# Chunk update of a recurrent layer: loops written out, the first slab's terms formed one step earlier, next terms in front of a slab's transposes, unread products left out

## The chip, the cores and the metric

The kernel runs on 1 core of one Trainium2 chip. The metric is the device time of one execution in microseconds (us). Before the change it is 9437.5 us, the median of three runs (9432.24, 9437.5 and 9437.68).

## What is computed

A small audio tower: a token layer, an attention layer, a feed-forward layer with top-k selection, a recurrent layer and a layer of experts, each added to a residual. The change touches the recurrent layer alone. Cut to what matters:

```python
def _mlp(params, z):
    W0, W1, P0, P1 = params
    h = z @ W0 + z @ P0
    h = jax.nn.silu(h)
    return h @ W1 + h @ P1
...
def step(carry, xs):
    cp, cm = carry
    k_t, v_t, q_t, a_t, th_t, e_t = xs
    g = jax.vmap(jax.grad(loss_fn))(cp, k_t, v_t)
    s = lambda c: c[:, :, None]
    nm = jax.tree_util.tree_map(lambda m, gg: m * s(e_t) - s(th_t) * gg, cm, g)
    np_ = jax.tree_util.tree_map(lambda p, m: p * (1.0 - s(a_t)) + m, cp, nm)
    out_t = jax.vmap(_mlp, in_axes=(0, 0))(np_, q_t)
    new_carry = jax.lax.stop_gradient((np_, nm))
    return (new_carry, out_t)
...
h = h + _L1_attn_ref(_layernorm(h, axis=-1), ...)
```

Each of 249 time steps takes a gradient of a two-layer network with respect to its own weights, updates momentum and weights with it, and evaluates the new network. All in float32.

## The kernel before, in words

The function recurrent_layer (L1801 on) doesn't update the weights at every step. It cuts the 249 steps into 16 chunks, 15 of 16 steps and a last one of 9. Within a chunk, a step works with the weights as they stood at the chunk's start and adds the contribution of the chunk's earlier steps from a history (tile hist: h, y and slope rows of the steps so far). At the start of the next chunk an **update** folds the whole history into weights and momentum. So the program is: update, 16 steps, update, 16 steps, and so on. All engines have their own instruction list for this and meet by counting semaphores: V counts what VectorE (DVE) has finished, T TensorE (PE), A ScalarE (ACT), P GpSimd (POOL). Each has a fixed number of counts per update and per step, so a wait is "V has reached the count of sn of slab 3 of chunk c".

The update goes over 16 slabs X, each of two halves k:

- DVE weighs history rows for a group of two slabs (weighed, L2503, tile wy, which lies in the buffer named hdiag), PE multiplies them with the history (new_terms, L2266, into the banks psNew, two pairs used in turn; a wait at its start asks for the sn of slab X - 2).
- DVE updates the slab with the result: sa (L2521), sb (L2527), sn (L2531), two instructions each, and between slabs makes the tables of decay factors for the chunk (beside, L2465 to L2498).
- PE turns the updated slab over (turned, L2282, transposes into the banks psC), and ACT copies it to where the steps read it (L2192).
- After slabs 4, 6, 8 and 10, PE forms base values for the steps from the chunk's slopes (from_last, L2305 in chunk 0, L2307 later), ACT copies them (L2200), SP and POOL store them (L2055). When all are stored, SP loads the first step's two base rows back (load_base, L2026 and L2027).
- After slab 12 PE turns the decay tables over (L2317, L2326). From these DVE makes cu (L2539), which the next chunk's update reads, then x0 from the two base rows (L2541), the first hidden activations (L2546, ACT's sigmoid L2204, L2551), PE turns them over (turn, L2336), DVE places them on a diagonal (L2556), and the first step's products begin (L2350).

PE issues the slabs in the order: transposes of X, from_last if there is one, new terms of X + 2. In front of each slab's transposes stands one product that nobody reads (kept_warm, L2250, 256 columns, into a psC bank); two more of 512 columns stand behind the last copy wait of the update and two more behind the definition of the step, ahead of the first turn (four in a row in the list).

A step is bound by PE: products with the chunk's weights (L2350), with the history, and backwards (L2403). Its last part on DVE is slope(0) and slope(1) (L2623, L2625, L2630, and L2634, which writes tile dl); SP copies h, y and dl of each step to the history in eight transfers each (to_hist, L2038) and stores y (L2160).

DVE's chunks 0 to 14 are one loop on the chip (Fori) and chunk 15 is written out behind it. PE has chunk 0, a loop over chunks 1 to 8, one over 9 to 14, and chunk 15. In a chunk, 15 steps are a loop and the last step is written out.

Of the kernel before, what the change touches and what calls it, by code (L numbers as in the profile page):

```python
# [7 lines left out]
ALU = mybir.AluOpType  # L8
# [7 lines left out]
CH, NCH = 16, 16  # L16
# [1766 lines left out]
def recurrent_layer(nc, CT, DXD, VR, GR, YR, BASED, BASEO, W0, P0, W1, P1):  # L1783
# [8 lines left out]
    with ExitStack() as ctx:  # L1792
# [3 lines left out]
        def sem(name):  # L1796
            return ctx.enter_context(nc.semaphore(name))
# [67 lines left out]
        psC, psBase, psOld = (b[6], b[0]), (b[3], b[4]), b[1][:, HD:]  # L1865
        psNew = ((b[5], b[7]), (b[1], b[2]))

        def slab(X, k):
# [7 lines left out]
                  5: ["rep0", "rep1"], 6: ["d3a", "d3b", "d3c"], 13: ["cm", "cmx"]}  # L1876
        vec_u = ["wy0"]
        for X in range(16):
# [11 lines left out]
        for X in range(16):  # L1890
            pe_u += [f"tr{X}0", f"tr{X}1"] + ([f"nb{X // 2 - 2}"] if X in NB else []) + ([f"nw{X + 2}"] if X < 14 else []) + (["ct", "cb"] if X == 12 else [])
        pe_s = ["tr", "pred", "gt", "yp", "yt", "ob", "a", "dd", "dt", "dha", "e", "tra", "dhb"]
# [8 lines left out]
        old_in = [Stages(sem(f"old_in{nb}"), [], ["in"], 16 * (1 + 2 * nb), first) for first, last, nb in PARTS]  # L1901
        old_out = Stages(sem("old_out"), [], ["out"], 16)
        slopes_out = Stages(sem("slopes_out"), ["out"], [], 8 * 16)
        ctn_in = Stages(sem("ctn_in"), ["in"], [], 8 * 16, 1)
# [9 lines left out]
        hist_d = Stages(sem("hist_d"), [], ["d"], 16 * NH)  # L1914
        for q in (*old_in, old_out, slopes_out, ctn_in, first_in, *base_out[0], *base_out[1], gates_in, cc_in, al_in, base_in, value_in, hist_h, hist_y, hist_d):
            q.base = 0
# [152 lines left out]
        with nc.Block() as block:  # L2069
# [173 lines left out]
            def _(e):  # L2243
                def chunk(c, steps, part):
# [6 lines left out]

                    def new_terms(X):

                        G = X // 2
                        e.wait_ge(V.sem, V.upd(c, f"wy{G}"))
                        if X == 0:

                            e.wait_ge(hist_h.sem, c * (hist_h.unit * CH))
                        if X >= 2:

                            e.wait_ge(V.sem, V.upd(c, f"sn{X - 2}1"))
                        for w in range(2):
                            for k in range(2):
                                j, m, g, n = slab(X, k)
                                rows = slice(32 * g, 32 * g + 32)
                                mm = e.matmul(psNew[X % 2][k][:, HD * w:HD * w + HD], wy[rows, G % 2, w, :, :].rearrange("p u d -> p (u d)"),  # L2266
                                              hist[rows, m * 4 + j, 0:HD], start=True, stop=True)
                        mm.then_inc(T.sem, 1)

                    def turned(X):  # L2270
                        for k in range(2):
                            if X:
                                e.wait_ge(A.sem, A.upd(c, f"c{X - 1}{k}1"))
                            if k == 0:
                                kept_warm(psC[k], 1, 256)
                        for k in range(2):
                            j, m, g, n = slab(X, k)
                            e.wait_ge(V.sem, V.upd(c, f"sn{X}{k}"))
                            for hf in range(2):
                                for w in range(2):  # L2280
                                    o = 256 * hf + 128 * w
                                    mm = e.transpose(psC[k][:, o:o + 128], mvt[:, 4 * n + j, HD * w + 128 * hf:HD * w + 128 * hf + 128], ident[:, :])  # L2282
                            mm.then_inc(T.sem, 1)

                    def from_last(q):
# [22 lines left out]
                        mm.then_inc(T.sem, 1)  # L2308

                    e.wait_ge(V.sem, V.begun(c))  # L2310
                    e.wait_ge(A.sem, A.begun(c))
                    settled(e, s_pe)
                    new_terms(0)
                    new_terms(1)
                    for X in range(16):
                        turned(X)
                        if X in NB:  # L2317
                            from_last(X // 2 - 2)
                        if X < 14:
                            new_terms(X + 2)  # L2320
                        if X == 12:
                            e.wait_ge(V.sem, V.upd(c, "d3c"))
                            e.wait_ge(A.sem, A.upd(c, "bs7"))
                            settled(e, s_pe)
                            for w in range(2):
                                mm = e.matmul(psCT[:, 128 * w:128 * w + 128], rep[:, w, :, :].rearrange("p i s -> p (i s)"), ident[:, :],  # L2326
                                              start=True, stop=True)
                            mm.then_inc(T.sem, 1)
                            for w in range(3):
                                mm = e.matmul(psH[:, 128 * w:128 * w + 128], ones[:, :], d3[w], start=True, stop=True)  # L2330
                            mm.then_inc(T.sem, 1)
                    e.wait_ge(A.sem, A.upd(c, "c1511"))
                    kept_warm(psC[0], 2)
                    def turn(hf, need):
# [95 lines left out]

                    kept_warm(psC[0], 2)
                    e.wait_ge(T.sem, T.upd(c, "cb"))
# [4 lines left out]
                    with e.Fori(0, steps - 1) as s:  # L2437
                        step(s, False)
                    step(steps - 1, True)

                chunk(0, CH, 0)
                for part in (1, 2):
                    with e.Fori(*PARTS[part][:2]) as c:
                        chunk(c, CH, part)
                chunk(NCH - 1, LAST, 3)

            @block.vector
            def _(e):
# [3 lines left out]
                def chunk(c, steps):  # L2452
# [48 lines left out]
                    def weighed(G):  # L2501
                        j, m = G // 2, G % 2
                        go(e.tensor_tensor(wy[:, G % 2, :, :, :],  # L2503
                                           hist[:, m * 4 + j, HD:HD + D].unsqueeze(1).unsqueeze(1).to_broadcast([128, 2, 2, D]),
                                           cmx[:, :, j, m, :].unsqueeze(3).to_broadcast([128, 2, 2, D]), ALU.mult), f"wy{G}")
# [64 lines left out]
                    def step(s, last):  # L2570
# [49 lines left out]
                        def slope(hf, names, need):  # L2620
# [34 lines left out]

                with e.Fori(0, NCH - 1) as c:
                    chunk(c, CH)
                chunk(NCH - 1, LAST)

# [81 lines left out]
```

## Time and profile before

| | before |
|---|---|
| runs, us | 9432.24, 9437.5, 9437.68 |
| profiled execution: its own time, us | 9434.71 |
| profiled execution: span from first to last instruction, us | 9432.9 |
| PE busy | 8531.5 us, 90% of the span |
| DVE busy | 4381.6 us, 46% |
| ACT busy | 1955.9 us, 21% |
| mean granted clock of TensorE | 0.951 |

The recurrent layer takes some 6.45 ms of the span: the first new terms start at 1944.9 us (L2266), the last chunk's first step at 8209.4 us. One chunk is some 412 to 417 us long, of which the update, from the last dl of one chunk to the first L2350 of the next, is 60.5 to 64.4 us in chunks 1 to 14, and 56.4 us in chunk 15.

### The profile page before, as it was taken

Reading aid. Unit: us, or ns where it says so; the run is one execution under the profiler, and the core shown is the slowest. Engines: PE = TensorE matmul, PEld = TensorE weight load, DVE = VectorE, ACT = ScalarE, POOL = GpSimd, SP = SyncE. Lnnn points to the kernel's source line nnn. Section 1 sums busy time; section 2 is a strip of 40 time slices with the busy share of each in tenths; the row PEclk is TensorE's granted clock in tenths of the full one; section 3 lists DMA queues with packets and bytes.
Section 4 is the critical chain, followed back from the end, with each engine's and each line's share of the span. In section 5 each row is a group of like instructions: output and inputs, shape, how many; then the busy total and the mean of one; then the engine's idle time right before and its main releaser. Section 6 shows DMA issues by size and latency. Waiting matters only on the chain. (4 is left out here: it accounts for less than half of the span.)

```text
span 9432.9 us, 368730 instructions
## 1 busy us (share of the span) xinstructions
PE 8531.5 (90%) x152997; PEld 5630.7 (60%) x152997; DVE 4381.6 (46%) x12189; ACT 1955.9 (21%) x4831; POOL 684.5 (7%) x844
## 2 busy tenths in 40 slices
PE   6888847679999999999999999999999999989999
PEld 2555515356667676666767666676767667653333
DVE  5455578853443444344344434434443444432222
ACT  1344425111111111111111111111111111113333
POOL 0000043110000000000000000000000000000000
PEclk8899966989999999999999999999999999989999
DMA  4000001721221212122122212222222222210000
GB/s 166 20 4 5 4 9 54 157 58 30 59 61 54 59 57 58 55 60 60 55 59 57 58 55 78 79 84 79 81 77 85 78 72 85 68 28 10 14 14 8
DMA packets 800576, 531.23 MB, mean 56 GB/s; under 512 B 277694, under 2 KB 789590, under 8 KB 797990
## 3 DMA queue, kind: packets, MB, share of 16 engines
q1 hardware_dynamic: 769046, 456.94, 17.6%
q0 software_dynamic: 30992, 67.51, 2.5%
q8 instruction: 289, 4.73, 0.2%
q14 instruction: 249, 2.04, 0.1%
HBM read 311.32 MB, written 175.89 MB: 52 GB/s over the span
## 5 line engine op out<-in xcount | busy, mean ns | idle before, releaser
L2350 PE MATMUL bank<-mv,hdiag 128*32 128x144 f32 x63744 | 2050.5, 286 | 9.9 <-DVE hdiag L2556 5.9
L2350 PEld LDWEIGHTS bank<-mv,hdiag 128*32 128x32 f32 x63744 | 1932.8, 110 | 88.7 <-DVE hdiag L2556 11.4
L2403 PE MATMUL bank<-mvt,ydiag 128*32 128x256 f32 x31872 | 1946.9, 381 | 0.0
L2403 PEld LDWEIGHTS bank<-mvt,ydiag 128*32 128x32 f32 x31872 | 1048.0, 110 | 565.5 <-issue 3.3
L2204 ACT ACTIVATE work<-work 128x128 f32<-128x128 f32 x498 | 154.4, 310 | 2211.7 <-DVE work L2546 2209.6
L2590 DVE TENSOR_TENSOR rep<-bank,ta 128x128 f32<-128x128 f32 x249 | 72.7, 292 | 994.9 <-PE bank L2350 994.9
L617 DVE TENSOR_REDUCE att_mx<-att_bank 124x2 f32<-124x496 f32 x512 | 334.0, 664 | 344.8 <-PE att_bank L422 344.8
L2623 DVE TENSOR_SCALAR work<-bank,ta 128x128 f32<-128x128 f32 x498 | 174.8, 351 | 592.0 <-PE bank L2403 592.0
L2192 ACT ACTIVATE mv<-bank 128x256 f32<-128x256 f32 x1024 | 313.7, 388 | 632.5 <-PE bank L2282 632.3
L2077 POOL MEMSET hdiag<- 128x1124 f32 x16 | 16.6, 1035 | 5391.0 <-DVEq L2647 5381.0
L2266 PE MATMUL bank<-hist,hdiag 32*128 32x256 f32 x2048 | 310.6, 456 | 97.3 <-DVE hdiag L2503 97.3
L1425 ACT ACTIVATE moe_hw<-moe_bank 128x496 f32<-128x496 f32 x512 | 271.2, 581 | 610.1 <-PE moe_bank L1339 610.0
L536 ACT ACTIVATE att_ex<-att_bank 124x496 f32<-124x496 f32 x512 | 283.8, 581 | 540.1 <-PE att_bank L434 540.1
L1473 DVE TENSOR_TENSOR moe_xc<-moe_xT,moe_bank 128x496 f32<-128x496 f32 x128 | 86.0, 672 | 620.4 <-PE moe_bank L1348 620.4
L2219 ACT ACTIVATE yth<-ydiag 64x32 f32 (+1 forms) x498 | 131.1, 263 | 1124.2 <-PE bank L2396 1112.9
L2214 ACT ACTIVATE mv<-hdiag 128x128 f32 (+1 forms) x249 | 106.3, 427 | 1219.9 <-PE bank L2350 1219.9
L2282 PE MATMUL bank<-r_ident,mvt 128*128 128x128 f32 x2048 | 297.3, 293 | 22.5 <-DVE mvt L2531 22.4
L422 PE MATMUL att_bank<-att_ka,att_qn 32*124 32x496 f32 x1024 | 293.4, 646 | 20.7 <-DVE att_mx L617 8.4
L2371 PE MATMUL bank<-hist,adiag 128*32 128x256 f32 x3984 | 309.4, 381 | 0.0
L2282 PEld LDWEIGHTS bank<-r_ident,mvt 128*128 128x128 f32 x2048 | 262.0, 152 | 67.8 <-DVE mvt L2531 41.4
L2266 PEld LDWEIGHTS bank<-hist,hdiag 32*128 32x128 f32 x2048 | 187.7, 213 | 179.2 <-issue 89.1
L1337 PE MATMUL moe_bank<-moe_xc,moe_w1T 64*128 64x496 f32 x1024 | 293.4, 636 | 0.8 <-DVE moe_xc L1473 0.8
(417 smaller groups left out, 11813.6 us busy)
## 6 DMA issues: line engine op xcount, KB each, us to landing
ring<-between_slopes SPq DMA_DIRECT2D x320, 512.0 KB, 4.1
baset<-between_base_old SPq DMA_DIRECT2D x265, 128.0 KB, 2.1
baset<-between_base SPq DMA_DIRECT2D x265, 128.0 KB, 2.2
hist<-h SPq DMA_DIRECT2D x1992, 8.0 KB
hist<-y SPq DMA_DIRECT2D x1992, 2.0 KB
hist<-dl SPq DMA_DIRECT2D x1992, 8.0 KB
between_base_old<-bo SPq DMA_DIRECT2D x240, 128.0 KB
ct<-between_table SPq DMA_DIRECT2D x320, 64.0 KB, 2.0
```

The source lines that it names most:

```text
L422: e.matmul(bank[i % 2][0:TL, 0:2 * L], qn[rows, t.buf(1), TL * a:TL * a + TL], ka[rows, t.buf(1), :, :], start=True, stop=True).then_inc(T ...
L536: e.activation(ex[:, t.buf(0), TILE_HEAD[i], :, :], bank[2 + i % 2][0:TL, 0:2 * L].rearrange("p (m n) -> p m n", m=2), ACT.Exp).then_inc(A ...
L617: e.tensor_reduce(mx[:, a, 32 * g + 16:32 * g + 18], bank[i % 2][0:TL, 0:2 * L].rearrange("p (h m) -> p h m", h=2), AX, ALU.max).then_inc( ...
L1337: e.matmul(dst[q], w1T[rows[q], x_, half], xc[rows[q], (I // 2) % 2, :], start=True, stop=False)
L1425: e.activation(hw[:, I % 4, q, :], bank[2 + 2 * (I % 2) + q][:, 0:2 * L], ACT.Relu).then_inc(A.sem, 1)
L2192: e.activation(dst, src, ACT.Copy).then_inc(A.sem, 1)
L2266: mm = e.matmul(psNew[X % 2][k][:, HD * w:HD * w + HD], wy[rows, G % 2, w, :, :].rearrange("p u d -> p (u d)"), hist[rows, m * 4 + j, 0:HD ...
L2282: mm = e.transpose(psC[k][:, o:o + 128], mvt[:, 4 * n + j, HD * w + 128 * hf:HD * w + 128 * hf + 128], ident[:, :])
L2350: mm = e.matmul(psP[32 * j:32 * j + 32, 0:MW], hdiag[:, hf, r, j, :], mv1[:, hf, r, j, :], start=(hf == 0 and r == 0), stop=(hf == 1 and r ...
L2371: mm = e.matmul(psA[32 * j:32 * j + 32, :], adiag[:, m, j, :], hist[:, m * 4 + j, HD + D:], start=(m == 0), stop=(m == 1))
L2403: mm = e.matmul(psBack[hf][32 * j:32 * j + 32, :], ydiag[:, n, j, :], both, start=(n == 0), stop=(n == 7))
L2623: nm(e.tensor_scalar(dh[:, half], S2, W16, None, ALU.mult))
```

## The change

It makes four edits to recurrent_layer.

1. The chunk loops of PE and DVE are written out in Python: c is a constant in each of 16 copies of the chunk. The loops over steps stay. ACT, POOL and SP are as before.
2. The next chunk's first weighed rows are formed in the last step of a chunk, in front of slope(0), behind a wait for ACT's copy of h and for the last y rows and the y store to have landed. They have a semaphore of their own (first_rows). PE forms new_terms(0) of the next chunk at the end of its list for the last step, and the two pairs of psNew banks are swapped.
3. In the update the new terms of X + 2 stand in front of the transposes of X, and from_last behind them.
4. All calls of kept_warm are gone. The transposes of X wait once for the last copy of X - 1, where two waits stood, one for each half.

```diff
-        psNew = ((b[5], b[7]), (b[1], b[2]))
+        psNew = ((b[1], b[2]), (b[5], b[7]))
...
                     def turned(X):
-                        for k in range(2):
-                            if X:
-                                e.wait_ge(A.sem, A.upd(c, f"c{X - 1}{k}1"))
-                            if k == 0:
-                                kept_warm(psC[k], 1, 256)
+                        if X:
+                            e.wait_ge(A.sem, A.upd(c, f"c{X - 1}11"))
...
+                    if part == 0:
+                        new_terms(0)
                     e.wait_ge(V.sem, V.begun(c))
                     e.wait_ge(A.sem, A.begun(c))
                     settled(e, s_pe)
-                    new_terms(0)
                     new_terms(1)
                     for X in range(16):
+                        if X < 14:
+                            new_terms(X + 2)
                         turned(X)
                         if X in NB:
                             from_last(X // 2 - 2)
-                        if X < 14:
-                            new_terms(X + 2)
...
                     e.wait_ge(A.sem, A.upd(c, "c1511"))
-                    kept_warm(psC[0], 2)
...
-                    kept_warm(psC[0], 2)
...
                     step(steps - 1, True)
-
-                chunk(0, CH, 0)
-                for part in (1, 2):
-                    with e.Fori(*PARTS[part][:2]) as c:
-                        chunk(c, CH, part)
-                chunk(NCH - 1, LAST, 3)
+                    if c + 1 < NCH:
+                        e.wait_ge(A.sem, A.begun(c + 1))
+                        e.wait_ge(hist_h.sem, (c + 1) * (hist_h.unit * CH))
+                        new_terms(0, c + 1)
+
+                for first, last, part in (*PARTS, (NCH - 1, NCH, 3)):
+                    for c in range(first, last):
+                        chunk(c, CH if c + 1 < NCH else LAST, part)
...
+                    if c == 0:
+                        weighed(0)
                     e.wait_ge(T.sem, T.begun(c))
                     e.wait_ge(A.sem, A.begun(c))
-                    e.wait_ge(hist_y.sem, c * (hist_y.unit * CH))
-                    weighed(0)
...
+                        if last and c + 1 < NCH:
+                            e.wait_ge(A.sem, A.step(c, s, "ht"))
+                            e.wait_ge(hist_y.sem, (c + 1) * (hist_y.unit * CH))
+                            weighed(0)
                         slope(0, ("dh1a", "dh2a", "dh3a", "da"), "dha")
...
-                with e.Fori(0, NCH - 1) as c:
-                    chunk(c, CH)
-                chunk(NCH - 1, LAST)
+                for c in range(NCH):
+                    chunk(c, CH if c + 1 < NCH else LAST)
```

How the order of the instructions moves, at three places. A row is a line of the kernel, an operation, its tiles and its shape; REGISTER_ALU rows compute the value of a wait, and ISA rows are waits and semaphore counts.

DVE, from a chunk's last slope to the next chunk's first slab, before (dl is the slope's result, L2503 the weighed rows, L2521 the first sa):

```order
L2630 TENSOR_TENSOR work<-work,bank 128x128
L2450 REGISTER_ALU
L2634 TENSOR_TENSOR dl<-work 128x128
L2450 REGISTER_ALU
L2647 ISA
L2656 REGISTER_ALU
L2656 COMPARE_AND_BRANCH
L2503 TENSOR_TENSOR hdiag<-hist,cmx 128x256
L2521 SCALAR_TENSOR_TENSOR mvt<-mvt,cu,bank 128x256 x2
L2503 TENSOR_TENSOR hdiag<-hist,cmx 128x256
L2527 SCALAR_TENSOR_TENSOR mvt<-mvt,cu 128x256 x2
```

The same place in the changed kernel, from the last step's slope(0) on (L2637 writes dl, L2524 is the first sa):

```order
L2621 TENSOR_TENSOR ddiag<-bank,mi 128x8x2x8
L2502 TENSOR_TENSOR hdiag<-hist,cmx 128x256
L2626 TENSOR_SCALAR work<-bank,ta 128x128
L2628 SCALAR_TENSOR_TENSOR work<-bank,ta,work 128x128
L2633 TENSOR_TENSOR work<-work,bank 128x128
L2637 TENSOR_TENSOR dl<-work 128x128
L2646 ISA
L2626 TENSOR_SCALAR work<-bank,ta 128x128
L2628 SCALAR_TENSOR_TENSOR work<-bank,ta,work 128x128
L2633 TENSOR_TENSOR work<-work,bank 128x128
L2637 TENSOR_TENSOR dl<-work 128x128
L2654 ISA
```

The weighed rows have moved from behind the loop's branch to a place two slopes earlier, and sa follows the last ISA row with no branch and no weighed rows between.

PE, from a chunk's last products backwards into the next update, before (chunk 15's copy, which stands behind the loop; L2266 are new terms, four products to a slab, L2250 the unread product, L2282 the transposes):

```order
L2403 MATMUL bank<-mvt,ydiag 32x256 x8
L2443 REGISTER_ALU
L2443 COMPARE_AND_BRANCH
L2443 UNCONDITIONAL_BRANCH
L2443 ISA
L2311 ISA
L2255 REGISTER_ALU
L2258 REGISTER_ALU
L2266 MATMUL bank<-hist,hdiag 128x256 x8
L2250 MATMUL bank<-yth,r_ident 128x256
L2278 REGISTER_ALU
L2282 MATMUL bank<-r_ident,mvt 128x128 x4
```

And now, at any chunk's end:

```order
L2401 MATMUL bank<-mvt,ydiag 32x256 x32
L2267 MATMUL bank<-hist,hdiag 128x256 x12
L2280 MATMUL bank<-r_ident,mvt 128x128 x8
L2267 MATMUL bank<-hist,hdiag 128x256 x4
L2280 MATMUL bank<-r_ident,mvt 128x128 x8
L2267 MATMUL bank<-hist,hdiag 128x256 x4
L2280 MATMUL bank<-r_ident,mvt 128x128 x8
```

The new terms of slabs 0, 1 and 2 now stand ahead of the first transposes (twelve products in one row), those of X + 2 ahead of the transposes of X, and the row of the unread product and the register rows are gone.

PE, from the update's last transposes to the first step, before (L2336 is the turn of h, L2350 the step's first products):

```order
L2282 MATMUL bank<-r_ident,mvt 128x128 x4
L2332 REGISTER_ALU
L2250 MATMUL bank<-yth,r_ident 128x512 x4
L2432 ISA
L2335 REGISTER_ALU
L2336 MATMUL bank<-r_ident,h 128x128
L2435 REGISTER_ALU
L2437 UNCONDITIONAL_BRANCH
L2437 ISA
L2343 ISA
L2350 MATMUL bank<-mv,hdiag 32x144 x44
```

And now:

```order
L2267 MATMUL bank<-hist,hdiag 128x256 x4
L2280 MATMUL bank<-r_ident,mvt 128x128 x24
L2334 MATMUL bank<-r_ident,h 128x128
L2434 UNCONDITIONAL_BRANCH
L2434 ISA
L2341 ISA
L2348 MATMUL bank<-mv,hdiag 32x144 x44
```

Between the last transposes and the turn of h stands nothing any more.

## Rows read from the trace of the kernel before

**Rows 1.** The page's busy times: engine, busy us, share of the span, instructions.

```profile
PE 8531.5 (90%) x152997; PEld 5630.7 (60%) x152997; DVE 4381.6 (46%) x12189; ACT 1955.9 (21%) x4831; POOL 684.5 (7%) x844
```

**Rows 2.** PE by line and shape: busy us, mean ns, idle before and its releaser.

```profile
L2266 PE MATMUL bank<-hist,hdiag 32*128 32x256 f32 x2048 | 310.6, 456 | 97.3 <-DVE hdiag L2503 97.3
L2282 PE MATMUL bank<-r_ident,mvt 128*128 128x128 f32 x2048 | 297.3, 293 | 22.5 <-DVE mvt L2531 22.4
L2250 PE MATMUL bank<-yth,r_ident 128*128 128x256 f32 x512 | 196.1, 468 | 5.0 <-ACT mv L2192 5.0
L2307 PE MATMUL bank<-hist,hdiag 32*32 32x256 f32 x1920 | 65.5, 380 | 0.0
```

**Rows 3.** DVE by line and shape, same columns.

```profile
L2503 DVE TENSOR_TENSOR hdiag<-hist,cmx 128x256 f32<-128x256 f32 x128 | 53.6, 419 | 51.1 <-issue 49.7 <-PEq L1932 0.9 <-DVEq L2647 0.5
```

**Rows 4.** Timeline, chunk 2 to 3: start us, us, engine, line, operation [idle before <-releaser].

```profile
3174.43 0.35 DVE L2623 TENSOR_SCALAR work<-bank,ta 128x128 f32<-128x128 f32 x1 [1.60 <-PE bank L2403]
...
3176.47 0.37 SPq L2160 DMA_DIRECT2D between_recurrent<-y  x1
...
3179.83 0.29 DVE L2634 TENSOR_TENSOR dl<-work 128x128 f32<-128x128 f32 x1
...
3183.64 0.42 DVE L2503 TENSOR_TENSOR hdiag<-hist,cmx 128x256 f32<-128x256 f32 x1 [3.51 <-issue]
...
3184.20 2.11 PE L2266 MATMUL bank<-hist,hdiag 32*128 32x256 f32 x16 [5.52 <-DVE hdiag L2503]
...
3186.31 0.87 DVE L2521 SCALAR_TENSOR_TENSOR mvt<-mvt,cu,bank 128x256 f32<-128x256 f32 x2 [2.25 <-PE bank L2266]
...
3188.76 1.97 PE L2282 MATMUL bank<-r_ident,mvt 128*128 128x128 f32 x8 [1.30 <-DVE mvt L2531]
...
3190.66 2.07 PE L2266 MATMUL bank<-hist,hdiag 32*128 32x256 f32 x8
...
3192.66 1.22 PE L2250 MATMUL bank<-yth,r_ident 128*128 128x256 f32 x2
```

**Rows 5.** Timeline, chunk 14 to 15, which DVE enters without a branch back.

```profile
8153.03 0.29 DVE L2634 TENSOR_TENSOR dl<-work 128x128 f32<-128x128 f32 x1
...
8153.79 0.43 DVE L2503 TENSOR_TENSOR hdiag<-hist,cmx 128x256 f32<-128x256 f32 x1 [0.46 <-DVEq L2647]
...
8155.45 0.87 DVE L2521 SCALAR_TENSOR_TENSOR mvt<-mvt,cu,bank 128x256 f32<-128x256 f32 x2 [1.24 <-PE bank L2266]
```

**Rows 6.** Stretches: us, busy PE, PEld, DVE, ACT, POOL, PE clock, DMA share, GB/s.

```profile
3186.31:3221.05 34.74, 33.44 (x278) 23.50 (x279) 31.76 (x89) 15.59 (x46) 8.88 (x16) 0.85 0.21 45
8155.45:8188.63 33.18, 31.01 (x278) 21.62 (x279) 31.68 (x89) 15.48 (x46) 11.96 (x22) 0.95 0.23 50
3183.24:3196.65 13.41, 11.15 (x50) 7.73 (x52) 9.81 (x30) 2.63 (x8) 7.82 (x15) 0.50 0.22 28
8159.65:8163.06 3.41, 3.41 (x14) 2.19 (x10) 3.41 (x9) 0.81 (x3) 2.86 (x6) 0.50 0.40 31
```

**Rows 7.** Timeline, PE in two slabs of chunk 3 at full clock.

```profile
3204.78 1.13 PE L2266 MATMUL bank<-hist,hdiag 32*128 32x256 f32 x8
...
3207.35 1.13 PE L2266 MATMUL bank<-hist,hdiag 32*128 32x256 f32 x8
```

**Rows 8.** Timeline, end of chunk 3's update and its first step.

```profile
3236.29 0.43 DVE L2541 TENSOR_TENSOR xb<-baset 128x256 f32<-128x256 f32 x1
...
3237.58 3.70 PE L2250 MATMUL bank<-yth,r_ident 128*128 128x512 f32 x8 [0.86 <-ACTq L2231]
...
3238.05 0.29 DVE L2551 TENSOR_TENSOR h<-work 128x128 f32<-128x128 f32 x1 [0.85 <-ACT work L2204]
...
3241.11 0.27 PE L2336 MATMUL bank<-r_ident,h 128*128 128x128 f32 x1
...
3242.03 2.90 PE L2350 MATMUL bank<-mv,hdiag 128*32 128x144 f32 x88 [0.64 <-DVEq L2566]
```

**Rows 9.** What the 16 instructions of L2541 waited for: us, times.

```profile
  DMA baset<-between_base: 3.4, 4
```

More of the change, by code:

```diff
@@ L1876, in recurrent_layer @@
                   5: ["rep0", "rep1"], 6: ["d3a", "d3b", "d3c"], 13: ["cm", "cmx"]}
-        vec_u = ["wy0"]
+        vec_u = []
         for X in range(16):
@@ L1890, in recurrent_layer @@
         for X in range(16):
-            pe_u += [f"tr{X}0", f"tr{X}1"] + ([f"nb{X // 2 - 2}"] if X in NB else []) + ([f"nw{X + 2}"] if X < 14 else []) + (["ct", "cb"] if X == 12 else [])
+            pe_u += ([f"nw{X + 2}"] if X < 14 else []) + [f"tr{X}0", f"tr{X}1"] + ([f"nb{X // 2 - 2}"] if X in NB else []) + (["ct", "cb"] if X == 12 else [])
         pe_s = ["tr", "pred", "gt", "yp", "yt", "ob", "a", "dd", "dt", "dha", "e", "tra", "dhb"]
@@ L1902, in recurrent_layer @@
         old_out = Stages(sem("old_out"), [], ["out"], 16)
+        first_rows = Stages(sem("first_rows_weighed"), ["wy0"], [])
         slopes_out = Stages(sem("slopes_out"), ["out"], [], 8 * 16)
@@ L1914, in recurrent_layer @@
         hist_d = Stages(sem("hist_d"), [], ["d"], 16 * NH)
-        for q in (*old_in, old_out, slopes_out, ctn_in, first_in, *base_out[0], *base_out[1], gates_in, cc_in, al_in, base_in, value_in, hist_h, hist_y, hist_d):
+        for q in (*old_in, old_out, first_rows, slopes_out, ctn_in, first_in, *base_out[0], *base_out[1], gates_in, cc_in, al_in, base_in, value_in, hist_h, hist_y, hist_d):
             q.base = 0
@@ L2250, in kept_warm, with new_terms @@
                             e.matmul(out[:, 0:cols], ident[:, :], yth[:, :, :].rearrange("p a s -> p (a s)")[:, 0:cols], start=True, stop=True)
-                    def new_terms(X):
+                    def new_terms(X, c=c):
                         G = X // 2
-                        e.wait_ge(V.sem, V.upd(c, f"wy{G}"))
-                        if X == 0:
-                            e.wait_ge(hist_h.sem, c * (hist_h.unit * CH))
+                        if G == 0:
+                            e.wait_ge(first_rows.sem, c + 1)
+                        else:
+                            e.wait_ge(V.sem, V.upd(c, f"wy{G}"))
                         if X >= 2:
@@ L2502, in weighed @@
                         j, m = G // 2, G % 2
-                        go(e.tensor_tensor(wy[:, G % 2, :, :, :],
-                                           hist[:, m * 4 + j, HD:HD + D].unsqueeze(1).unsqueeze(1).to_broadcast([128, 2, 2, D]),
-                                           cmx[:, :, j, m, :].unsqueeze(3).to_broadcast([128, 2, 2, D]), ALU.mult), f"wy{G}")
+                        ins = e.tensor_tensor(wy[:, G % 2, :, :, :],
+                                              hist[:, m * 4 + j, HD:HD + D].unsqueeze(1).unsqueeze(1).to_broadcast([128, 2, 2, D]),
+                                              cmx[:, :, j, m, :].unsqueeze(3).to_broadcast([128, 2, 2, D]), ALU.mult)
+                        if G == 0:
+                            ins.then_inc(first_rows.sem, 1)
+                        else:
+                            ins.then_inc(V.sem, 1)
+                    if c == 0:
+                        weighed(0)
                     e.wait_ge(T.sem, T.begun(c))
                     e.wait_ge(A.sem, A.begun(c))
-                    e.wait_ge(hist_y.sem, c * (hist_y.unit * CH))
-                    weighed(0)
                     for X in range(16):
```

## The prediction

> **What bounds the kernel now.** I read the page's busy times first: PE is busy for 90% of the span and every other engine for under half [rows 1]. That share is mostly the steps, which the change leaves alone. So I looked for what the update waits for, chunk by chunk, in the views by line, the timeline, and the busy time of single stretches.
>
> The first wait is at each chunk's start. By line, the weighed rows L2503 have 49.7 us of idle DVE in front of them that nothing in the profile ends, "issue" [rows 3]. It is in 14 places, so 3.55 us each. In chunk 3 it stands between dl and the weighed rows, 3.51 us; PE waits 5.52 us in all, its products begin at 3184.20, and the first sa starts 6.48 us after dl began (3186.31 less 3179.83) [rows 4]. Chunk 15, which DVE enters without a branch back, has 0.46 us in that place and 2.42 us from dl to sa [rows 5]. So I read the 3.5 us as the loop's jump; the rest is the weighed rows, the new terms, and a half clock.
>
> The second is the pace of the slabs. From sa of slab 0 to sn of slab 10 chunk 3 takes 34.74 us and chunk 15 33.18, and DVE is busy for 31.76 and 31.68 of them, PE for 33.44 and 31.01 [rows 6]. Both engines are nearly full. In chunk 3 the granted clock was 0.50 from 3183.24 to 3196.65, after PE's idle time; in chunk 15, after a shorter idle time, only from 8159.65 to 8163.06 [rows 6]. At half clock a slab costs PE 2.07 + 1.22 + 1.97 = 5.26 us [rows 4]; at full clock slabs follow each other after 2.57 us [rows 7].
>
> The third is the end of the update. The hidden activations h are written by 3238.34, but PE stands in four unread products for 3.70 us, turns h at 3241.11, and starts the step at 3242.03 [rows 8].
>
> **The change part by part**, for one chunk, then times the chunks. The sum is made against the profiled execution, 9434.7 us, which is 2.8 us under the median.
>
> *Loops written out, first terms formed early.* The jump, the weighed rows and PE's new terms leave the way from dl to sa. What is left is dl itself (0.29) and DVE's sequence of about 0.46, as in chunk 15 [rows 5]: 0.8 against 6.48, so 5.7 less. Against that stands the new wait. The y store of the last step is issued until 3176.84, while slope(0) began at 3174.43 [rows 4]; the weighed rows and slope(0) behind them now start when the store has landed, and with slope(0) 1.6 us and wy 0.42 long slope(1) may be pushed. The trace has no such wait. Its bounds are 0 (slope(1) waits for PE until 3178.74 anyway) and 1.5 us (landing 1.5 us after issue). I take 0.5. PE is not held up: in the last step its own list waits for no slope. So 5.2 less, in 14 chunks 73 us. Chunk 15 had no jump and gains 2.42 less 1.3, 1 us.
>
> *Unread products between slabs, and the order of terms and transposes.* The 512 rows of unread products cost 196.1 us [rows 2], 0.77 us in each of 256 slabs, 1.22 at half clock [rows 4]. Without them PE needs 2.1 us a slab at full clock (terms 1.13 [rows 7], transposes half of 1.97 [rows 4]; the means of [rows 2], 1.21 and 1.16 for eight rows, mix both levels), and DVE becomes the limit: 31.7 us busy for these eleven slabs. The gain is then at most 34.74 less 31.7, 3 us a chunk. At half clock PE needs 4.04 us a slab, 1.2 less than before, but it stays the limit, and each further slab at half clock costs 4.04 less 2.57, 1.5 us, and every from_last another 1.1 (65.5 us in 60 groups [rows 2]). So the two ends of this term are 3 us less, and, were all eleven slabs at half clock, 11 x 4.04 + 4 x 2.18 = 53.2 us against 34.74, 18 us more. What decides is for how long the clock stays down. In the trace it came back after three slabs with the unread products in them, with PE full. I take a stretch two slabs and one from_last longer: 3 x 1.2 less, 2 x 1.5 + 1.1 more, about 0. It is nearest to the row of 13.41 us at 0.50.
>
> The Trainium skill speaks against this part: "TensorE: Matmul & The Clock Gate" says in its section on what matters for kernels that gaps in PE's work bring the clock back to its lower level, and in Part 4 that transposes don't count as work in the same way. In this kernel an idle time of 5.5 us was indeed followed by a half clock [rows 4, 6]; on transposes no row here separates them.
>
> *Base rows.* Slabs that run faster bring x0 nearer to the chain from_last, ACT's copy, store, load. L2541 waited for that load in 4 of 16 chunks already [rows 9], and from_last now stands behind one more set of new terms (1.1 us). So what DVE gains behind slab 10 is lost at x0; I take 0.6 more, with ends 0 and 2: 8 us.
>
> *Unread products at the end.* With h there at 3238.34 and 0.92 us from turn to step as now, the step would start at 3239.3 in place of 3242.03 [rows 8]: 2.7 less in each of 16 chunks, 43 us. The cover that they gave is gone: PE is idle from the last transposes to the step, some 3 us but for the turn, and the clock may be down at the step's start. One stretch at half clock was 3.41 us long [rows 6] and would lose 1.7 us of a full PE; bounds are 0 and two stretches, 3.4. I take 2.2, 35 us. So of this part little is left.
>
> *Two waits in one, register rows, swapped banks.* The second copy's wait is the later one, and covered by DVE's pace: nothing. The ISA rows of PE's list lie in front of waits: nothing. Between the ends of POOL's and SP's lists nothing moves; POOL's clearing of a buffer is released by dl as before, and read after slab 0.
>
> Sum: -73 - 1 + 0 + 8 - 43 + 35 = -74, and 9434.7 - 74 = 9360.7; I say **9361 us**, 0.8% faster.
>
> **The rivals.**
>
> *Full clock, DVE as the limit.* PE's idle time at the boundary falls from 5.5 us to one or two, and the clock may hardly fall. For it: chunk 15 lost one stretch of 3.41 us alone [rows 6]. Against: it had the unread products. Then slabs go as in chunk 15, 34.74 less 33.18, 1.6 us, in 14 chunks 22 us, up to 3 in the best case, and the step's start loses nothing (35): -74 - 22 - 35, or about 9304 us. Chance 0.23.
>
> *Half clock through the update: slower.* The place is PE from slab 0 on. Without the unread products it has gaps in each slab while DVE sets the pace, and once the clock is down it needs all its time for 4.04 us a slab. For it: in the trace the clock was at 0.50 for 13.41 us even with the unread products. Against: at half clock PE is full, as it was when the clock rose. If the half clock lasts for all slabs, the term is up to 18 us a chunk in place of 0; with two thirds of it, 12 in 15 chunks, it is 180 us: 9541. It decides from 5 us a chunk on (74 over 15): with 1.5 us a slab and 1.1 for every second one, that is two or three slabs more at half clock than the five I took, some eight of sixteen. Chance 0.15; the cases about that point, where gain and loss cancel, have 0.11. By the skill's rule on gaps and transposes this rival would be the likely one.
>
> *The end's gain is given back at x0.* If the base rows land two us later than DVE could use them, the term of 0.6 becomes 2: 20 us more, 9381. For it: four waits already [rows 9]. Chance 0.1, on the same side.
>
> *The jump stays in another form.* A list twice as long might stall DVE once a chunk at its start as the loop's branch did, 3.5 us x 14 = 50 us: 9411. Against it: chunk 15's start is straight code, and had 0.46 us [rows 5]. Chance 0.05. The Trainium skill, "Runtime: NRT & Kernel Launch", section on instruction fetch, says that a taken branch outside the window already fetched stalls, and straight code is fetched ahead; chunk 15's start agrees.
>
> **How the numbers follow.** The forecast has a chance of 0.36, full clock 0.23, x0 0.10, the jump 0.05, the cancelling case 0.11, half clock 0.15. A measurement of this kernel tells some 0.2% from no change, 19 us. Faster by more than that are the first four, 0.74; the same 0.11; slower 0.15. The range of 8 in 10 runs from 9295, a little beyond the full clock case, to 9450, which takes in the cancelling case and leaves the half clock outside.
>
> **What would show it.** Right: no idle DVE over 1 us between the last dl and sa of slab 0; new terms of slab 0 done ahead of dl; from dl to the first product of a step about 57 us where it was 62.2; h turned within half a us of its writing. The clock's rows at the boundary show which case holds: 0.50 for some five slabs is mine, 1.00 the first rival, 0.50 up to slab 15 the second. Wrong: idle DVE in front of sa that PE ends over many slabs, sn of slab 10 over 38 us behind the first sa, an L2350 group of a step's start at half clock for more than two stretches, or a last dl over 1.5 us late.

## The result, and the profile after

The changed kernel takes 9616.95 us (median of four runs, 9602.86 to 9626.0) against 9434.87 us (four runs, 9424.21 to 9437.68): a ratio of 1.0194, with a 95% interval of 1.0176 to 1.0211. It is slower by 182 us where 74 us less were forecast. The profiled execution took 9626.0 us, its span is 9624.5 us, and its mean granted clock 0.907, where it was 0.951.

The page's busy times of the changed kernel, to set beside [rows 1]:

```profile
PE 8738.3 (91%) x152357; PEld 5747.5 (60%) x152357; DVE 4377.2 (45%) x12189; ACT 1975.4 (21%) x4831; POOL 683.8 (7%) x844
```

PE executes 640 instructions fewer (the 320 unread products are two instructions each) and is busy for 207 us more. By line and shape (columns as in [rows 2]):

```profile
L2267 PE MATMUL bank<-hist,hdiag 32*128 32x256 f32 x2048 | 493.0, 628 | 72.0 <-DVE ta L2464 26.4 <-DVEq L2654 23.2 <-DVE hdiag L2502 22.3
L2280 PE MATMUL bank<-r_ident,mvt 128*128 128x128 f32 x2048 | 461.9, 400 | 27.7 <-ACT mv L2193 26.8 <-DVE cu L2542 0.9
L2305 PE MATMUL bank<-hist,hdiag 32*32 32x256 f32 x1920 | 117.5, 630 | 0.0
```

The same number of terms, transposes and from_last products as before, each longer: 628 ns in the mean against 456, 400 against 293, 630 against 380. DVE's sa now waits for them, 300.6 us where it was 108.5 (first row, of the kernel before); the weighed rows have lost their 49.7 us of "issue" and wait for the y store:

```profile
L2521 DVE SCALAR_TENSOR_TENSOR mvt<-mvt,cu,bank 128x256 f32<-128x256 f32 x512 | 221.7, 474 | 109.8 <-PE bank L2266 108.5
```

```profile
L2524 DVE SCALAR_TENSOR_TENSOR mvt<-mvt,cu,bank 128x256 f32<-128x256 f32 x512 | 222.1, 474 | 305.2 <-PE bank L2267 300.6 <-DVEq L2654 4.5
...
L2502 DVE TENSOR_TENSOR hdiag<-hist,cmx 128x256 f32<-128x256 f32 x128 | 53.4, 417 | 81.5 <-DMA between_recurrent<-y 81.1 <-PEq L1933 0.5
```

The timeline of the changed kernel from chunk 2 to chunk 3, and of its slabs, in the columns of [rows 4]:

```profile
3221.16 0.43 DVE L2502 TENSOR_TENSOR hdiag<-hist,cmx 128x256 f32<-128x256 f32 x1 [5.95 <-DMA between_recurrent<-y]
...
3221.74 1.13 PE L2267 MATMUL bank<-hist,hdiag 32*128 32x256 f32 x8 [0.67 <-DVE hdiag L2502]
...
3224.12 0.29 DVE L2637 TENSOR_TENSOR dl<-work 128x128 f32<-128x128 f32 x1
...
3224.72 0.87 DVE L2524 SCALAR_TENSOR_TENSOR mvt<-mvt,cu,bank 128x256 f32<-128x256 f32 x2 [0.30 <-DVEq L2654]
...
3231.55 2.08 PE L2267 MATMUL bank<-hist,hdiag 32*128 32x256 f32 x8
...
3235.46 2.08 PE L2267 MATMUL bank<-hist,hdiag 32*128 32x256 f32 x8
```

From dl to sa it is now 0.60 us where it was 6.48 [rows 4]. But slabs follow each other after 3.91 us (3235.46 less 3231.55) where it was 2.57 [rows 7]. Why, the stretches of chunk 3's update show (columns of [rows 6]; from sa of slab 0 to the end of sn of slab 10, the half clock alone, and from there to x0):

```profile
3224.72:3267.58 42.86, 41.03 (x240) 27.45 (x248) 32.12 (x88) 14.02 (x40) 11.72 (x21) 0.52 0.15 34
3226.67:3288.11 61.44, 60.47 (x346) 40.73 (x347) 38.98 (x107) 21.46 (x60) 18.53 (x33) 0.50 0.23 55
3267.58:3292.94 25.36, 23.78 (x154) 16.37 (x138) 13.48 (x36) 9.76 (x28) 9.83 (x14) 0.60 0.37 96
```

The clock is at 0.50 for 61.44 us, with PE busy for 60.47 of them; in the kernel before it came back after 13.41 us [rows 6]. At full clock, DVE's 32.12 us of work in the first stretch would be the limit; at half clock PE's 41.03 us are.

It comes back at 3288.11, 4.83 us ahead of x0, just behind the turn of the decay tables, which starts here:

```profile
3285.84 1.06 PE L2325 MATMUL bank<-r_ident,rep 128*128 128x128 f32 x4
```

In all 16 chunks the clock rose 0.8 to 3.6 us after the first of these products. They are the first in the update that are neither terms, transposes nor from_last.

In the mean of chunks 1 to 14, from the timelines (starts, but for sn of slab 10 its end):

| us a chunk | before | after |
|---|---|---|
| last dl to first sa | 6.57 | 0.59 |
| first sa to sn of slab 10 | 35.27 | 42.86 |
| sn of slab 10 to x0 | 15.46 | 25.37 |
| x0 to the first L2350 / L2348 | 5.51 | 3.83 |
| the steps, to the last dl | 351.16 | 351.42 |

That is 10.1 us a chunk or 142 us in 14; chunk 0 is 20 us longer, chunk 15 18 us, and some 12 us lie ahead of the layer and behind it, where the code is the same: 192 us of span.

### The profile page after: what moved, and what is told of

It reads as the page before. It is cut to its first block and busy times, and to the rows that moved or that the text cites. A ratio compares the mean times of both kernels' runs of the same rounds, so it can differ in the third digit from the quotient of the medians.

```text
span 9624.5 us, 364466 instructions
## 1 busy us (share of the span) xinstructions
PE 8738.3 (91%) x152357; PEld 5747.5 (60%) x152357; DVE 4377.2 (45%) x12189; ACT 1975.4 (21%) x4831; POOL 683.8 (7%) x844
## 5 line engine op out<-in xcount | busy, mean ns | idle before, releaser
L2348 PE MATMUL bank<-mv,hdiag 128*32 128x144 f32 x63744 | 2072.0, 288 | 8.5 <-DVE hdiag L2559 6.3
L2348 PEld LDWEIGHTS bank<-mv,hdiag 128*32 128x32 f32 x63744 | 1947.8, 111 | 88.1 <-DVE hdiag L2559 9.1
L2401 PE MATMUL bank<-mvt,ydiag 128*32 128x256 f32 x31872 | 1923.9, 381 | 0.4 <-issue 0.4
L2401 PEld LDWEIGHTS bank<-mvt,ydiag 128*32 128x32 f32 x31872 | 1024.0, 110 | 564.5 <-issue 0.9
L2267 PE MATMUL bank<-hist,hdiag 32*128 32x256 f32 x2048 | 493.0, 628 | 72.0 <-DVE ta L2464 26.4
L2280 PE MATMUL bank<-r_ident,mvt 128*128 128x128 f32 x2048 | 461.9, 400 | 27.7 <-ACT mv L2193 26.8
L2280 PEld LDWEIGHTS bank<-r_ident,mvt 128*128 128x128 f32 x2048 | 367.3, 208 | 175.8 <-issue 91.1
L2267 PEld LDWEIGHTS bank<-hist,hdiag 32*128 32x128 f32 x2048 | 285.5, 299 | 227.4 <-issue 81.0
L2524 DVE SCALAR_TENSOR_TENSOR mvt<-mvt,cu,bank 128x256 f32<-128x256 f32 x512 | 222.1, 474 | 305.2 <-PE bank L2267 300.6
```

What stands on the lines that cost most here:

```text
L2348: mm = e.matmul(psP[32 * j:32 * j + 32, 0:MW], hdiag[:, hf, r, j, :], mv1[:, hf, r, j, :], start=(hf == 0 and r == 0), stop=(hf == 1 and r ...
L2401: mm = e.matmul(psBack[hf][32 * j:32 * j + 32, :], ydiag[:, n, j, :], both, start=(n == 0), stop=(n == 7))
```

## The experiments

Theory: the unread products between slabs bring the clock back, and without them it stays down. Rival: the new order of terms and transposes, or the early first terms, hold PE up. In the runs with unread products the two waits of each slab's transposes come back with them.

**Unread products put back.** Three versions of the changed kernel: all of them, those between slabs, those at the end.

```diff
                     def turned(X):
-                        if X:
-                            e.wait_ge(A.sem, A.upd(c, f"c{X - 1}11"))
+                        for k in range(2):
+                            if X:
+                                e.wait_ge(A.sem, A.upd(c, f"c{X - 1}{k}1"))
+                            if k == 0:
+                                kept_warm(psC[k], 1, 256)
...
                     e.wait_ge(A.sem, A.upd(c, "c1511"))
+                    kept_warm(psC[0], 2)
...
+                    kept_warm(psC[0], 2)
                     e.wait_ge(T.sem, T.upd(c, "cb"))
```

> The changed kernel with all unread products back (one of 256 columns in front of each slab's transposes, four of 512 at the end); loops written out, early first terms and the new order stay. Theory (the unread products alone bring the clock back up in an update): granted clock 1.00 after some 14 us of each update as in the kernel before, sa of slab 0 to sn of slab 10 at 33 to 35 us where the changed kernel has 42.9, last dl to first step 55 to 57 us where it has 72.5, total about 9325 us. Rival (terms in front of the transposes, or the early first terms, keep the clock down or PE waiting): clock 0.50 for about 61 us of each update still, total 9600 us or more.

The next has the first hunk of this diff alone, the third the two hunks at the end alone.

> The changed kernel with the 256-column unread product back in front of each slab's transposes, none at the end. Theory: clock up in the update as with all of them; the end of the update is 2 to 3 us shorter per chunk than with all of them, 9285 to 9325 us. If the products at the end were what held the clock for the step: a stretch of half clock at each step 0, and the end's gain given back, 9325 to 9345 us.

> The changed kernel with the four 512-column unread products at the update's end back, none between slabs. Theory (the products between slabs are what counts): clock 0.50 for about 61 us of each update as in the changed kernel, end of the update 2 us longer, about 9640 us. If the end's products were what was missing (rival): clock back up in the update, under 9450 us.

And the converse, the kernel before without its products between slabs:

```diff
-                        for k in range(2):
-                            if X:
-                                e.wait_ge(A.sem, A.upd(c, f"c{X - 1}{k}1"))
-                            if k == 0:
-                                kept_warm(psC[k], 1, 256)
+                        if X:
+                            e.wait_ge(A.sem, A.upd(c, f"c{X - 1}11"))
```

> The kernel before with the unread product between slabs left out and the one wait in place of two; loops, first terms, order and the products at the end as before. Theory: the clock stays at 0.50 through each update, sa of slab 0 to sn of slab 10 at 43 us or more where it had 35, total 9560 to 9680 us. Rival (it is the new order or the early first terms): clock as before, DVE the limit, 9390 to 9435 us.

Measured: all back 9345.56 us (ratio to the kernel before 0.9905, 0.9888 to 0.9921); between slabs alone 9318.15 (0.9878, 0.9861 to 0.9894); at the end alone 9645.08 (1.0214, 1.0197 to 1.0231); the kernel before without those between slabs 9737.28 (1.032, 1.0303 to 1.0337), 57 us more than its theory allowed. The stretch from sa of slab 0 to x0 of chunk 3, columns of [rows 6], first with the products between slabs, then the kernel before without them:

```profile
3161.93:3212.50 50.57, 48.07 (x418) 34.53 (x418) 45.78 (x124) 23.48 (x71) 21.54 (x35) 0.93 0.32 77
```

```profile
3248.85:3317.40 68.55, 64.97 (x378) 44.15 (x378) 46.73 (x124) 24.13 (x69) 17.50 (x28) 0.54 0.25 64
```

PE does more products in less time: 48.07 us at a mean clock of 0.93 against 64.97 at 0.54. The products between slabs are worth 9645 less 9346, 299 us, in the changed kernel and 9737.3 less 9436.8 (the kernel before, run beside it), 301 us, in the kernel before: the same, whatever the order. The rival falls. The four at the end cost 27 us (9346 less 9318). Put together, the changed kernel with all of them is 91 us faster than the kernel before; 299 us more and 27 less make 181 us more, and 182 were measured.

**The parts of the change that save.** Loops written out alone, in the kernel before (for PE; DVE's loop in the same way), and the changed kernel with all unread products and the old order:

```diff
-                chunk(0, CH, 0)
-                for part in (1, 2):
-                    with e.Fori(*PARTS[part][:2]) as c:
-                        chunk(c, CH, part)
-                chunk(NCH - 1, LAST, 3)
+                for first, last, part in (*PARTS, (NCH - 1, NCH, 3)):
+                    for c in range(first, last):
+                        chunk(c, CH if c + 1 < NCH else LAST, part)
```

> The kernel before with the chunk loops of PE and DVE written out and nothing else. Theory (the 3.55 us at 14 chunk starts are the loop's jump, and the steps of chunks 1 to 8 go 0.22 us faster with constants in the waits, as in the changed kernel): idle DVE ahead of the first weighed rows 0.5 us in every chunk, last dl to sa of slab 0 about 2.5 us, 50 + 26 us less, 9350 to 9370 us. Rival (the faster steps come from another part, the swapped banks or the early first terms): 9380 to 9395 us, steps as before.

```diff
-                        if X < 14:
-                            new_terms(X + 2)
                         turned(X)
                         if X in NB:
                             from_last(X // 2 - 2)
+                        if X < 14:
+                            new_terms(X + 2)
```

> The changed kernel with all unread products back and the old order too: transposes of X, from_last, then the terms of X + 2. Beside the run that had all unread products and the new order (9346 us): if the new order costs nothing but the later from_last, sn of slab 10 to x0 falls from 18.5 to 15.5 us and sa of slab 0 to sn of slab 10 grows from 33.4 to 35 us, 9325 to 9345 us. If the new order is what lets the clock come back sooner: half clock of 14 to 17 us in each update and 9360 us or more.

Measured: 9316.47 us (0.9875, 0.9859 to 0.9892) and 9321.01 us (0.9873, 0.9856 to 0.9889). The loops alone give 118 us, more than their theory. The weighed rows by line in that run:

```profile
L2501 DVE TENSOR_TENSOR hdiag<-hist,cmx 128x256 f32<-128x256 f32 x128 | 53.7, 420 | 5.5 <-DVEq L2645 4.9 <-PEq L1932 0.6
```

The 49.7 us of "issue" [rows 3] are gone: they were the loop's jump. From dl to sa it is 2.52 us in the mean, 4.05 less, 57 us in 14 chunks. A step of chunks 1 to 8 takes 21.59 us from slope to slope in place of 21.84 (medians), 15 such in 8 chunks, 30 us. And at the starts of chunks 3 to 9 the clock didn't fall, with 2.24 to 2.60 us of idle PE in place of some 5.5; the first 17.66 us behind dl in chunk 3 (columns of [rows 6]):

```profile
3152.34:3170.00 17.66, 13.45 (x98) 9.31 (x98) 16.12 (x46) 4.99 (x17) 9.19 (x17) 1.00 0.14 22
```

From sa to sn of slab 10 this gives another 1.6 us a chunk, 22 us. The length of one idle time doesn't decide it alone: at the other eight starts of this run the same 2.24 us stood, and the clock fell; in the changed kernel no idle time at a start is over 2.1 us, and it fell at all 15. The early first terms add nothing to it (9321 against 9316, ranges that overlap): dl to sa falls from 2.52 to 0.59, but the last dl itself comes 1.4 us later behind the wait for the y store, and the clock fell at 14 of 15 chunk starts again.

**Are the products needed to hold the clock, or only to raise it?** In the changed kernel, unread products in slabs 0 to 3 alone; and half as wide in all slabs:

```diff
-                            if k == 0:
+                            if k == 0 and X < 4:
                                 kept_warm(psC[k], 1, 256)
```

> The changed kernel with the 256-column unread product in front of the transposes of slabs 0 to 3 alone. If the unread products only bring the clock up, and it stays up without them: DVE becomes the limit after slab 4, last dl to first step 50 to 52 us, 9250 to 9285 us. If they are also what keeps it up: clock back to 0.50 from about slab 5 on, 1.5 us a slab more for some ten slabs, 9450 to 9560 us.

```diff
-                                kept_warm(psC[k], 1, 256)
+                                kept_warm(psC[k], 1, 128)
```

> The changed kernel with an unread product of 128 columns (half as wide) in front of each slab's transposes, none at the end. If that brings the clock up too: PE needs 0.35 us less a slab, DVE nearly the limit, 9270 to 9310 us. If it doesn't: clock 0.50 through the update, and each slab 0.6 us longer than in the changed kernel, 9700 to 9780 us.

Measured: 9295.43 us (0.9849, 0.9832 to 0.9865) and 9383.66 us (0.9939, 0.9922 to 0.9956). After slab 4 of the first version, in chunk 3, with terms, transposes and from_last alone:

```profile
3182.00:3208.00 26.00, 24.73 (x289) 17.41 (x287) 24.45 (x68) 16.31 (x48) 9.62 (x17) 1.00 0.38 100
```

The clock stays at 1.00 over 26 us of the same stream of work that the changed kernel does at 0.50 throughout. So the products are needed to raise it, and for a few slabs. The time is 10 us over what was expected for this case: x0 waited 31.5 us in all for the base rows, and in each of chunks 1 to 15 the clock fell once more about the step's start, from 46 us or more behind dl on, for 3.4 to 10.2 us. At half width the half clock lasted between 6.8 and 58 us, not the same from chunk to chunk: neither expectation. Both waits of each slab stand in this version too, so they aren't what brings the clock back in the versions above.

**Combinations.** The loops alone with products in slabs 0 to 3 (the edit above), with and without the four at the end, and the same pair with the early first terms:

```diff
-                    kept_warm(psC[0], 2)
```

> The kernel before with its chunk loops written out and unread products only in front of the transposes of slabs 0 to 3; the four at the end, the old order and the old place of the first terms stay. Against the loops written out alone (9316 us): if the clock stays up after slab 4 as with the new order, sa of slab 0 to sn of slab 10 falls from 33.7 to 32 us and the rest stays: 9285 to 9295 us. If in this order the clock falls after slab 4: 9400 us or more.

> As the run before it in this list, without the four unread products at the end. If the end's products only cost time: x0 to first step 2.7 us in place of 5.3, 9245 to 9255 us. If they hold the clock for step 0: first step to last dl grows by 2 to 4 us a chunk through half clock in step 0, 9280 to 9310 us.

> Loops written out and early first terms with the old order, unread products in slabs 0 to 3 and the four at the end. If the early first terms save what they take off the way from the last dl to sa (2.5 to 0.6 us) against the kernel of this list without them: 30 us less than that, about 9260 us. If the wait in front of slope(0) and a clock that falls more often give it back, as the pair 9316 and 9321 us suggests: within 15 us of it.

> As the third of this list without the four unread products at the end. Beside the run with the new order and the same unread products (9295 us) the base rows come earlier: sn of slab 10 to x0 15.3 in place of 16.3 us, 9270 to 9285 us. If the later transposes of the old order move the end of the update instead: 9295 us or more.

Measured: 9312.78, 9293.92, 9307.96 and 9302.02 us (ratios 0.9869, 0.9852, 0.9872 and 0.9862, each within 0.0017). All four lie within 20 us of 9295 us; the first met neither of its expectations, the others the second of theirs. In the first, with the old order, leaving out the products behind slab 3 gains nothing that can be told (9316 to 9313 us), and in chunk 3 the clock fell once more amid the slabs, 1.8 us after an idle time of PE of 1.62 us had ended, and stayed down for 13.7 us. Without the end's products x0 to first step falls from some 6.4 to 3.0 us and the steps, step 0 above all, grow by 2.1 to 2.6, so of the time 19 and 6 us remain, the second within the runs' spread. The early first terms are worth 5 us with the end's products and lose 8 without, nothing that can be told: the second reading of their expectation.

**What the new order costs with the clock up.** 9346 against 9321 us. DVE waited 32.9 us for the decay tables in the one and 9.9 in the other. The tables' turn ahead of slab 12's terms:

```diff
                     for X in range(16):
+                        if X == 12:
+                            e.wait_ge(V.sem, V.upd(c, "d3c"))
+                            e.wait_ge(A.sem, A.upd(c, "bs7"))
...
                         if X < 14:
                             new_terms(X + 2)
                         turned(X)
```

> The changed kernel with all unread products back and the new order, but with the decay tables' turn ahead of slab 12's terms and transposes, not behind them. With these products the new order was 24 us slower than the old one (9346 against 9321 us). Theory (what it costs is DVE's wait for the tables, 32.9 us against 9.9 over 16 chunks): the wait ahead of cm under 10 us in all, sn of slab 10 to x0 16 us or less in place of 18.5, 9315 to 9330 us. Rival (the later from_last and base rows hold x0): the wait goes, x0 then waits for the base rows, 9340 us or more.

> The same move in the version with unread products in slabs 0 to 3 alone and none at the end (9295 us). Theory: 1 to 2 us a chunk less, 9265 to 9285 us. Rival: base rows hold x0 at 16 us behind sn of slab 10, 9290 us or more.

Measured: 9342.16 us (0.9894, 0.9878 to 0.9911) and 9299.18 (0.9856, 0.9839 to 0.9872): no change in either. In the first, by line:

```profile
L2549 DVE TENSOR_TENSOR xb<-baset 128x256 f32<-128x256 f32 x16 | 6.8, 426 | 35.3 <-DMA baset<-between_base 35.3
L2498 DVE TENSOR_TENSOR rep<-bank,mi 128x128 f32<-128x128 f32 x16 | 4.5, 283 | 0.0
```

The wait for the tables is 0, and x0 waits 35.3 us for the base rows in its place: one wait stood in front of another. So from_last one slab earlier:

```diff
-        NB = (4, 6, 8, 10)
+        NB = (3, 5, 7, 9)
...
-                            from_last(X // 2 - 2)
+                            from_last(X // 2 - 1)
```

> All unread products, the new order, the tables' turn ahead of slab 12, and from_last one slab earlier (behind slabs 3, 5, 7 and 9). The run without that shift left DVE waiting 35.3 us for the base rows ahead of x0 and took 9342 us. If the base rows are what the new order costs with the clock up: that wait under 5 us, sn of slab 10 to x0 16 us or less, 9300 to 9315 us. If something behind it holds the end (hz, loads of the step): the wait goes and the time stays over 9330 us.

> The same shift with unread products in slabs 0 to 3 alone and none at the end (9299 us without the shift, 34.5 us of waits for base rows). If the base rows are the limit at the end there too: 9260 to 9275 us, the lowest of all versions. If not: 9285 us or more.

Measured: 9345.59 us (0.9904, 0.9887 to 0.992) and **9267.17 us** (0.9829, 0.9812 to 0.9845). The wait of x0 is down in both, in the second to this:

```profile
L2547 DVE TENSOR_TENSOR xb<-baset 128x256 f32<-128x256 f32 x16 | 6.8, 425 | 5.0 <-DMA baset<-between_base 4.6
```

With unread products in all slabs and at the end, the time doesn't move: x0 comes 3.2 us sooner behind slab 10, slab 10 itself comes 2.1 us later, and the step starts 2.1 us later behind x0. With few of them, the base rows were the limit, and the 32 us come out. What the 24 us of the new order are in the version with all products is thus not settled. The last version is the fastest: loops written out, early first terms, new order, unread products in slabs 0 to 3, the tables ahead of slab 12, from_last a slab earlier.

## Why the prediction was wrong, point by point

- *Loops written out, first terms formed early*, forecast 5.2 us less a chunk: 0.59 us from dl to sa was met (0.8 forecast), and the last dl is 1.4 us later against the last product in the mean (0.5 forecast, bound 1.5; single chunks have up to 3.3), 4.6 us net. The jump's part is right, 4.05 us measured alone. The early first terms' part, by the same sum some 1.1 us a chunk (2.42 less 0.8, less 0.5), didn't show in the time: 9321 us against 9316 without them. Not seen: that the steps of chunks 1 to 8 would each lose 0.25 us. The loops alone show it, so it comes with them (last section).
- *Unread products between slabs*, forecast 0: **this is the step that failed.** I let the half clock last for five slabs, because in the trace it ended after 13.41 us with PE full, and took PE being full for what had ended it. In its place: without these products PE was as full, 60.47 of 61.44 us, and the clock stayed at 0.50 until the turn of the decay tables behind slab 12. The term measured 299 and 301 us in two pairs of runs, 18.7 us a chunk. The second rival had the mechanism, at 12 us a chunk and a chance of 0.15; its 9541 us were 76 short. The cost was also booked over eleven slabs alone, 53.2 us at the worst: they measured 42.86, 7.6 more than before in the mean, and from sn of slab 10 to x0 the half clock cost another 9.9 us, where I had only 0.6 for base rows. The first rival's reason, that a short idle time would hardly let the clock fall, didn't hold either: no idle time at a start was over 2.1 us, and it fell at every one. The order of terms and transposes stood at nothing in the same term; with all unread products it went with 24 us more, with its cause open.
- *Base rows*, forecast 0.6: in the changed kernel x0 never waits for them, since half clock makes the slabs slower than the chain. With the clock up the third rival's mechanism is there: 35.3 us of waits, and 32 us back for moving from_last. Right in kind, and hidden here.
- *Unread products at the end*, forecast 2.7 less and 2.2 back: x0 to first step is 1.7 less; alone they measured 27 us of 16 chunks (9346 less 9318), 1.7 a chunk net, where I had 0.5. The stretch of half clock in step 0 that I had booked does come, in 10 of 16 chunks.
- *Two waits in one, registers, banks*: nothing showed against them; they weren't tried alone.
- *The jump in another form*: no. DVE's 5.5 us in all, above, bound it.

The Trainium skill, "TensorE: Matmul & The Clock Gate", section "Why this matters for your kernels", tells to keep the engine busy without a break to reach the upper level, and to leave no long gap, which brings the lower one back. The trace agrees on the fall after idle time (5.52 us in the kernel before); on the rise it doesn't, for this mix of products: 61.44 us at 0.50 with PE busy for 60.47. The remark on transposes in Part 4 of the same page of the Trainium skill fits, but no run here tells transposes from the terms over 32 rows beside them. In all 16 chunks the clock rose at the turn of the decay tables, whose products are neither; that they brought it back is likely and not shown, as no run moves them alone.

## What to carry to other kernels

A product that nobody reads may be what raises the clock: before leaving it out, look at the granted clock where it stands, and at which products ran just before each rise, and price its loss as every other product of the stretch at half clock, to the stretch's end. Where the clock only has to be raised, a few such products at the start are enough, and the rest can go (here 9318 to 9295 us; in the old order it made no difference). And when a wait is moved, look at which wait stands behind it: the tables' wait hid one of the same size for the base rows.

## What was not expected of the hardware

The same stream of terms, transposes and from_last stayed at the clock it was entered with: 0.50 for 61.44 us with PE busy for 60.47, 1.00 for 26 us with PE busy for 24.73 (with the one fall named above, in another version). A loop's jump on DVE cost 3.55 us at each of 14 chunk starts, and the clock fell at all of them; without the jump, it stayed up at seven. And in the steps of chunks 1 to 8 one group of products backwards is faster by 0.21 us with the chunk loops written out. A step of chunk 5 in the timeline, of the kernel before and of the changed one:

```profile
4231.93 0.49 PE L2390 MATMUL bank<-repl,y 128*128 128x128 f32 x2 [0.21 <-DVE y L2603]
...
4233.82 2.12 PE L2403 MATMUL bank<-mvt,ydiag 128*32 128x256 f32 x30
```

```profile
4302.03 0.49 PE L2388 MATMUL bank<-repl,y 128*128 128x128 f32 x2 [0.17 <-DVE y L2606]
...
4303.93 1.91 PE L2401 MATMUL bank<-mvt,ydiag 128*32 128x256 f32 x30
```

PE waits 0.04 us less for y, and the thirty products behind take 1.91 us, not 2.12. It isn't that constants are faster as such: chunks 9 to 14 were a loop too, and a step of chunk 11 takes 1.92 us for this group in both kernels. What slowed the loop over chunks 1 to 8 alone wasn't tried.
